# A fused vision block on one core: results with tokens on partitions, one set of value products moved behind the scores, all squares on the vector engine

## The chip, the core and the metric

The kernel runs on one core of a Trainium2 chip. The core has a matrix engine (TensorE, PE in the rows; PEld is its weight load), a vector engine (DVE), a scalar engine (ACT), GpSimd (POOL) and a sync engine (SP) that issues the transfers. The metric is device time in microseconds, the median of several runs. All times in the rows are microseconds from the start of one profiled execution.

## The reference

The input is 32 images of 3x64x64. Each is cut into 16 patches of 768 values, which makes 512 tokens. One block of a transformer follows, all of it in float32:

```python
h = patches @ W.T + b + pos_emb                # 512 x 768 @ 768 x 256
h = h + attention(layernorm(h))                # 16 heads of 16, causal, ALiBi bias, 16 tokens an image
h = h + ffn(layernorm(h))
# ffn: hid = bitlinear(x, w_fc) + gate * (x @ v.T @ fast_b.T @ u.T)     256 -> 1024
#      out = bitlinear(relu(hid) ** 2, w_proj)                          1024 -> 256
# bitlinear(x, w): s = mean(|w|, row); x @ (clip(round(w / s), -1, 1) * s).T
```

`s` of the last `bitlinear` has one value for each of the 256 output features, so it can be multiplied in after the product.

## The kernel before, in words

All 512 tokens are on the chip at once, as four blocks of 128 (`BLOCKS`) in two halves of 256 (`HALVES`, index `f`). Each engine has its program written out by hand, in the order in which it is to run; semaphores join the engines. There is no scheduler: an instruction whose semaphore is late holds everything behind it on its engine.

The order on PE: embedding; transposes of the normalised tokens `z`; key, query and value products of half 0; scores of half 0; key, query and value products of half 1; transposes of `u`; scores of half 1; `values(0)` (probabilities times values); transposes of the rounded weights; `project(0)`; `values(1)`; transposes of `z` and of the residual stream `h2` for half 0; the hidden layer (`hidden`, four steps `j` of 256 features); the output products `mlp_out(f, j)`, with the steps of half 1's hidden layer between them.

Products that need more accuracy than one pass has are split: an operand is held as a high part (`hi`, made by ACT) and a low part (`lo`, made by DVE or POOL by subtraction). So each hidden step `n = 4f + j` is followed by this chain: ACT applies relu and scale to the two PSUM tiles (`relus`); DVE or POOL squares the result in full precision (`square`); ACT makes the rounded square (`squares`, `sq_hi`); the same engine as for `square` subtracts (`square_low`, `sq_lo`); PE multiplies both parts by the weights `mlp_t` (`mlp_out`). POOL does n = 1, 2, 3 and DVE does n = 0, 4, 5, 6, 7 (`SQ_POOL`, `SQ_DVE`).

The result is held with the 256 features on the partitions and the tokens along the row, two tiles for each half. For that PE transposes `h2` of each half (`turn(f, h2, ...)`, line 311), DVE copies it out (`tokens_copy`, line 898), and DVE adds it to the scaled product in one instruction (`result`, line 877), with the scale as a value per partition. The host transposes the array that comes back.

`key_spread` lays the keys of each head of a group of four into their own rows; of the four heads of half 0 ACT does head 0, POOL head 1, DVE heads 2 and 3. `fold_v` (line 407) makes a 256x16 product of the low-rank factors `v` and `fast_b`; ACT copies it to `vf_sb`, and POOL makes `v_fold` from it.

The lines that follow are the functions that the change touches.

Of the kernel before, what the change touches and what calls it, by code (L numbers as in the profile page):

```python
# [7 lines left out]
F32 = mybir.dt.float32  # L8
# [6 lines left out]
P = 128  # L15
# [41 lines left out]
def build_program(nc, head, pos, tail, consts, w_q, w_k, w_v, w_fc, w_mlp, w_proj, proj_bias, u_t0, v_t0,  # L57
                  out_t):
    with ExitStack() as ctx:
# [3 lines left out]
        def sem(name):  # L63
# [16 lines left out]
        vf_sb = sb("vf_sb", [P, KE, RANK])  # L80
# [61 lines left out]
        h2_t = sb("h2_t", [P, HALVES, KE, HT])  # L142
# [8 lines left out]
        out_sb = tail_sb[:, :, :, :].rearrange("p b k t -> p (b k t)")[:, 0:HALVES * KE * HT].rearrange(  # L151
            "p (f m t) -> p f m t", f=HALVES, m=KE)
# [7 lines left out]
        vf_ps = bank[3][:, 0:KE * RANK]  # L160
# [6 lines left out]
        h2t_ps = [bank[3], bank[6]]  # L167
        low_ps = [bank[2][:, 0:HT], bank[4][:, 0:HT]]
        FCB = [bank[i] for i in (0, 1, 2, 0, 5, 1, 2, 0)]
        mlp_ps = [[bank[7][:, m * HT:(m + 1) * HT] for m in range(KE)],  # L170
                  [bank[3][:, 0:HT], bank[6][:, 0:HT]]]
# [32 lines left out]
        vf_done, vf_copied = sem("vf_done"), sem("vf_copied")  # L204
# [46 lines left out]
        h2t_turned = sem("h2t_turned")  # L251
        h2t_ready = sem("h2t_ready")
# [10 lines left out]
        out_ready = sem("out_ready")  # L263
# [6 lines left out]
        SQ_DVE, SQ_POOL = (0, 4, 5, 6, 7), (1, 2, 3)  # L270

        @block.sync
        def _(sp):
# [20 lines left out]
            for f in range(HALVES):  # L294
                for m in range(KE):
                    sp.wait_ge(out_ready, f * KE + m + 1)
                    sp.dma_start(out_t[m * P:(m + 1) * P, f * HT:(f + 1) * HT],
                                 out_sb[:, f, m, :]).then_inc(out_done, 16)
            sp.wait_ge(out_done, 16 * HALVES * KE)

        @block.tensor
        def _(pe):
# [170 lines left out]
            def mlp_out(f, j):  # L473
# [7 lines left out]
                order = [(a, m) for m in range(KE) for a in range(2)] if last else \  # L481
                    [(a, m) for a in range(2) for m in range(KE)]
                for a, m in order:
                    w = mlp_t[:, 2 * j + a, m * P:(m + 1) * P]
# [4 lines left out]
                    if last and a == 1 and m == 0:  # L489
                        mm.then_inc(mlp_tile, 1)  # L490
# [29 lines left out]
            fold_v()  # L520
# [12 lines left out]
            scores(1)  # L533
            pe.wait_ge(ut_ready, 2)
# [7 lines left out]
            pe.wait_ge(duo_ready, 3)  # L542
            project(0)
            turn_mlp(0)
# [4 lines left out]
            turn(0, h2, h2t_ps[0], h2_ready, h2t_turned)  # L549
# [24 lines left out]
            hidden_low(1, 0)  # L574
            hidden_low(1, 1)
# [543 lines left out]
```

## Time and profile before

| | |
|---|---|
| median of 3 runs | 73.71 us (73.63 to 75.11) |
| the profiled execution | 73.37 us, of which its span is 71.4 us |
| PE busy | 62.4 us, 87% |
| DVE busy | 44.5 us, 62% |
| ACT busy | 38.3 us, 54% |
| POOL busy | 31.9 us, 45% |
| granted TensorE clock, mean | 0.996 |

A busy share is an average over stages that have different limits. PE's share of 87% counts a matmul from its start to a modelled end, so neighbouring matmuls overlap in it; the distance between two starts tells more. The two rows for DVE and ACT say nothing on whether they are waited for; that stands in what ended PE's idle times.

### The profile page before, as it was taken

To read this page: it belongs to the slowest core of one execution; us is meant where nothing else is said; L and a number is where in the kernel's file an instruction comes from. 1 tells how busy PE (TensorE), PEld (TensorE's weight loads), DVE (VectorE), ACT (ScalarE), POOL (GpSimd) and SP (SyncE) were. 2 spreads that over 40 slices of the span, in tenths; PEclk is the share of its full clock that TensorE was granted. 3 is DMA by queue.
4 is the path that set the end of the run, shared out by engine and by line. 5 is a ranking of instruction groups with operands and counts; after the bars stand their busy time and mean duration, and the time that the engine had idled before them with its cause. 6 is when DMAs were issued, how large, how long until landed. Compare 5 with 4: busy or idle time off the path is not lost. (4 is left out here: it accounts for less than half of the span.)

```text
span 71.4 us, 2149 instructions
## 1 busy us (share of the span) xinstructions
PE 62.4 (87%) x890; PEld 56.0 (78%) x890; DVE 44.5 (62%) x94; ACT 38.3 (54%) x76; POOL 31.9 (45%) x44
## 2 busy tenths in 40 slices
PE   4999999999899999992969959999965899999840
PEld 3678788889799999991948839979855689999730
DVE  1000059288979849977989964368994216589970
ACT  5200005703859759673499895836660593897000
POOL 7400425898567279997994000000089089100000
PEclk9999999999999999999999999999999999999998
DMA  0999999999400000000000000000000000000044
GB/s 5 274 292 328 375 392 412 409 339 405 173 14 0 9 0 0 0 9 0 9 0 0 14 5 0 0 9 0 0 0 0 0 0 0 0 0 0 9 146 148
DMA packets 3497, 6.74 MB, mean 94 GB/s; under 512 B 400, under 2 KB 1312, under 8 KB 3488
## 3 DMA queue, kind: packets, MB, share of 16 engines
q1 hardware_dynamic: 3488, 6.60, 25.9%
q8 instruction: 7, 0.11, 0.7%
q14 instruction: 2, 0.02, 0.1%
HBM read 6.08 MB, written 0.52 MB: 93 GB/s over the span
## 5 line engine op out<-in xcount | busy, mean ns | idle before, releaser
L486 PE MATMUL psum<-sq_hi,mlp_t 128*128 128x256 f32 x32 | 8.1, 289 | 1.6 <-POOL sq_lo L1015 1.2
L594 ACT ACTIVATE std<-mv,eps_sb 128x1 f32<-128x1 f32 x8 | 2.2, 292 | 13.5 <-DVE mv L774 13.5
L1009 POOL TENSOR_TENSOR kqv_sb<-head_sb 128x512 f32<-128x512 f32 x3 | 3.2, 1062 | 13.5 <-ACT head_sb L720 13.5
L720 ACT ACTIVATE head_sb<-psum,fc_scale 128x256 f32<-128x256 f32 x16 | 6.5, 473 | 2.6 <-PE psum L465 2.6
L486 PE MATMUL psum<-sq_lo,mlp_t 128*128 128x256 f32 x32 | 7.8, 280 | 0.0
L486 PEld LDWEIGHTS psum<-sq_hi,mlp_t 128*128 128x128 f32 x32 | 6.0, 188 | 2.2 <-issue 2.2
L456 PE MATMUL psum<-zt_hi,fc_t 128*128 128x256 f32 x32 | 6.8, 285 | 0.3 <-ACT zt_hi L603 0.3
L770 DVE TENSOR_TENSOR h<-psum,pos_sb 128x256 f32<-128x256 f32 x4 | 1.6, 412 | 8.7 <-PE psum L305 8.7
L456 PE MATMUL psum<-zt_lo,fc_t 128*128 128x256 f32 x32 | 6.6, 279 | 0.0
L305 PE MATMUL psum<-head_sb 128*128 128x256 f32 x24 | 6.4, 431 | 0.0
L305 PEld LDWEIGHTS psum<-head_sb 128*128 128x128 f32 x24 | 5.1, 220 | 1.2 <-DMA head_sb<-head 0.5
L486 PEld LDWEIGHTS psum<-sq_lo,mlp_t 128*128 128x128 f32 x32 | 6.0, 188 | 0.0
L798 DVE TENSOR_TENSOR zt_lo<-psum,zt_hi 128x512 fp32r<-128x512 f32 x4 | 2.8, 691 | 5.2 <-ACT zt_hi L603 5.2
L456 PEld LDWEIGHTS psum<-zt_hi,fc_t 128*128 128x128 f32 x32 | 5.3, 188 | 0.6 <-issue 0.6
L305 PE MATMUL psum<-head_sb,tail_sb 128*128 128x256 f32 x24 | 5.5, 379 | 0.0
L780 DVE TENSOR_SCALAR z<-h,mv,rstd 128x256 f32<-128x256 f32 x8 | 5.2, 655 | 0.3
L456 PEld LDWEIGHTS psum<-zt_lo,fc_t 128*128 128x128 f32 x32 | 5.3, 188 | 0.0
L727 ACT ACTIVATE sq_hi<-head_sb 128x512 fp32r<-128x512 f32 x8 | 5.0, 636 | 0.1
L305 PEld LDWEIGHTS psum<-head_sb,tail_sb 128*128 128x128 f32 x24 | 4.5, 190 | 0.6
L1015 POOL TENSOR_TENSOR sq_lo<-kqv_sb,sq_hi 128x512 fp32r<-128x512 f32 x3 | 3.8, 1278 | 2.3 <-ACT sq_hi L727 2.3
L325 PE MATMUL psum<-zt_hi,kqv_hi 128*128 128x256 f32 x16 | 4.8, 299 | 0.0
L1021 POOL TENSOR_SCALAR fc_whole<-fc_sb,fc_scale 128x256 f32<-128x256 f32 x8 | 4.6, 598 | 0.0
(112 smaller groups left out, 169.4 us busy)
## 6 DMA issues: line engine op xcount, KB each, us to landing
head_sb<-head SPq DMA_DIRECT2D x6, 256.0 KB, 4.7
fc_sb<-w_fc SPq DMA_DIRECT2D x2, 512.0 KB, 6.7
mlp_sb<-w_mlp SPq DMA_DIRECT2D x2, 512.0 KB, 9.0
tail_sb<-tail SPq DMA_DIRECT2D x2, 384.0 KB, 5.8
out_t<-tail_sb SPq DMA_DIRECT2D x4, 128.0 KB, 1.8
pos_sb<-pos SPq DMA_DIRECT2D x1, 256.0 KB, 5.0
kqv_sb<-w_k SPq DMA_DIRECT2D x1, 256.0 KB, 6.0
kqv_sb<-w_q SPq DMA_DIRECT2D x1, 256.0 KB, 6.0
```

The costliest lines, as they stand in the source:

```text
L305: return pe.matmul(tok_ps[b], lhs, head_sb[:, k, HT:HT + E], start=k == 0, stop=k == KF - 1)
L325: mm = pe.matmul(ps[f][:, g * HT:(g + 1) * HT], w, part[f][:, k, :], start=k == 0 and i == 0, stop=k == KE - 1 and i == 2)
L456: pe.matmul(FCB[n][:, a * HT:(a + 1) * HT], fc_t[:, k, m * P:(m + 1) * P], part[f][:, k, :], start=a == 0 and k == 0 and part is z2t_hi, s ...
L486: mm = pe.matmul(mlp_ps[f][m], w, part[:, n % RING, a, :], start=j == 0 and a == 0 and i == 0 and (m == 0 or f == 1), stop=last and a == 1 ...
L594: nc.scalar.activation(std[:, which, b:b + 1], mv[:, which, b, 1:2], ACT.Sqrt, bias=eps_sb[:, 0:1]).then_inc(std_ready, 1)
L720: nc.scalar.activation(relu[:, n % PART_RING, a, :], FCB[n][:, a * HT:(a + 1) * HT], ACT.Relu, scale=fc_scale[:, 0, m:m + 1]).then_inc(rel ...
L727: nc.scalar.activation(sq_hi[:, n % RING, :, :], relu[:, n % PART_RING, :, :], ACT.Square).then_inc(sq_hi_ready, 1)
L780: dve.tensor_scalar(z[:, b, :], hidden_state[:, b, :], mv[:, which, b, 0:1], rstd[:, which, b:b + 1], ALU.subtract, ALU.mult).then_inc(z_s ...
L798: dve.tensor_tensor(dst, src, hi.bitcast(F32), ALU.subtract).then_inc(signal, 1)
L1009: pool.tensor_tensor(sq[:, r, :, :], relu[:, r, :, :], relu[:, r, :, :], ALU.mult).then_inc(sq_pool, 1)
L1015: pool.tensor_tensor(sq_lo[:, n % RING, :, :], sq[:, r, :, :], sq_hi[:, n % RING, :, :].bitcast(F32), ALU.subtract).then_inc(sq_lo_pool, 1)
L1021: pool.tensor_scalar(dst[:, m, :], w[:, m, :], scale[:, 1, m:m + 1], ROUND, ALU.mult, ALU.add).then_inc(signal, 1)
```

## The change

The change has six parts.

1. The result is made with tokens on the partitions. In `mlp_out` the squares are now the stationary operand and the weights move, as many products and of the same shape as before. The transposes of `h2`, DVE's copies of them and the host's transpose go away. The scale now varies along the row, so it needs a tile that has it in every partition: `fold_v_spread_scale` makes it with two float32 products of the broadcast scale with the identity, next to the old `fold_v`, and ACT copies both out together (`side_sb`, 128x288). The last step is two instructions for each of the four blocks: DVE multiplies by the scale, then POOL (blocks 0, 1) or DVE (blocks 2, 3) adds `h2`.
2. `fold_v` moves from before the scores of half 0 to just before `project(0)`, with the two products for the scale.
3. `value(1)` moves from before `turn_u` to between `scores(1)` and `values(0)`.
4. Head 2 of half 0's key spread moves from DVE to POOL; DVE's first `fc_sums` moves ahead of `zt_low(1)`.
5. DVE makes all eight squares and low parts. In half 0 it normalises blocks 2 and 3 first and squares after; in half 1 `square(n + 1)` stands ahead of `square_low(n)`.
6. PE, ACT: transposes of `z` of half 1 stand before `mlp_out(0, 0)`; `mlp_out(0, 1)` stands behind the first hidden step of half 1 and `mlp_out(0, 2)` behind its third. ACT runs `relus(1)` and `squares(1)` ahead of the standard deviations of blocks 2 and 3, and one standard deviation of half 0 ahead of `mlp_signs(0)`.

The diff, cut to its core:

```diff
-        SQ_DVE, SQ_POOL = (0, 4, 5, 6, 7), (1, 2, 3)
+        SQ_DVE, SQ_POOL = (0, 1, 2, 3, 4, 5, 6, 7), ()
...
-            def fold_v():
+            def fold_v_spread_scale():
                 pe.wait_ge(v0_in, 16)
+                pe.wait_ge(mlp_scaled, 1)
                 for k in range(KE):
-                    mm = pe.matmul(vf_ps[:, k * RANK:(k + 1) * RANK], v_sb[:, k * P:(k + 1) * P], v_sb[:, E:E + RANK],
+                    pe.matmul(side_ps[:, k * RANK:(k + 1) * RANK], v_sb[:, k * P:(k + 1) * P], v_sb[:, E:E + RANK],
+                              start=True, stop=True)
+                for m in range(KE):
+                    c = KE * RANK + m * P
+                    mm = pe.matmul(side_ps[:, c:c + P], mlp_scale[:, 0, m:m + 1].broadcast_to([P, P]), ident,
                                    start=True, stop=True)
-                mm.then_inc(vf_done, 1)
+                mm.then_inc(side_done, 1)
...
+                for a, b in order:
                     for i, part in enumerate((sq_hi, sq_lo)):
-                        mm = pe.matmul(mlp_ps[f][m], w, part[:, n % RING, a, :],
-                                       start=j == 0 and a == 0 and i == 0 and (m == 0 or f == 1),
+                        mm = pe.matmul(mlp_ps[f * BH + b], part[:, n % RING, a, b * P:(b + 1) * P],
+                                       mlp_t[:, 2 * j + a, :],
+                                       start=j == 0 and a == 0 and i == 0 and (b == 0 or f == 1),
                                        stop=last and a == 1 and i == 1, skip_group_check=True)
...
             value(0)
-            fold_v()
             score_bias(0)
             scores(0)
             pe.wait_ge(k_copied, 1)
             key(1)
-            pe.wait_ge(vf_copied, 1)
             query(1)
-            pe.wait_ge(q_copied, 1)
-            value(1)
             pe.wait_ge(shift_ready, 1)
             pe.wait_ge(v_copied, 1)
             turn_u()
             score_bias(1)
             scores(1)
+            value(1)
...
             pe.wait_ge(duo_ready, 3)
+            fold_v_spread_scale()
             project(0)
+            pe.wait_ge(side_copied, 1)
             turn_mlp(0)
...
             turn(0, z, z2t_ps[0], z2_ready, z2t_turned)
-            turn(0, h2, h2t_ps[0], h2_ready, h2t_turned)
...
             hidden(0, 3)
+            turn(1, z, z2t_ps[1], z2_ready, z2t_turned)
             pe.wait_ge(mlpt_ready, 2)
             mlp_out(0, 0)
-            mlp_out(0, 1)
-            pe.wait_ge(h2t_ready, 1)
-            turn(1, z, z2t_ps[1], z2_ready, z2t_turned)
-            turn(1, h2, h2t_ps[1], h2_ready, h2t_turned)
             hidden_main(1, 0, (z2t_hi,))
             low_rank(1)
             hidden_main(1, 0, (z2t_lo,))
+            mlp_out(0, 1)
+            hidden_low(1, 0)
+            hidden_main(1, 1)
+            hidden_low(1, 1)
             pe.wait_ge(relu_ready, 6)
-            hidden_main(1, 1)
-            hidden_low(1, 0)
-            hidden_low(1, 1)
+            hidden(1, 2)
             mlp_out(0, 2)
-            hidden(1, 2)
             pe.wait_ge(relu_ready, 8)
             hidden(1, 3)
             mlp_out(0, 3)
...
-            def result(f, m):
-                if f == 1 and m == 0:
+            def scale_result(b):
+                if b < BH:
+                    dve.wait_ge(mlp_step, STEPS)
+                elif b == BH:
                     dve.wait_ge(mlp_tile, 2)
                 else:
-                    dve.wait_ge(mlp_step, STEPS * (f + 1))
-                dve.wait_ge(h2t_ready, f + 1)
-                dve.scalar_tensor_tensor(out_sb[:, f, m, :], mlp_ps[f][m], mlp_scale[:, 0, m:m + 1],
-                                         h2_t[:, f, m, :], ALU.mult, ALU.add).then_inc(out_ready, 1)
+                    dve.wait_ge(mlp_step, 2 * STEPS)
+                dve.wait_ge(side_copied, 1)
+                dve.tensor_tensor(out_sb[:, b, :], mlp_ps[b], scale_row, ALU.mult).then_inc(out_scaled, 1)
+
+            def add_result(b):
+                dve.wait_ge(out_scaled, b + 1)
+                dve.tensor_tensor(out_sb[:, b, :], out_sb[:, b, :], h2[:, b, :], ALU.add).then_inc(out_dve, 1)
```

**Where instructions move.** First PE, from the last key and query products of half 1 to the transposes of the feed-forward weights. L345 (L344 after) is `value(1)`, L371 (L370) the scores, L389 (L388) `values(0)`. Before:

```order
L325 MATMUL psum<-zt_hi,kqv_hi 128x256 [waits zt_hi_ready,q_w_lo,zt_lo_ready,q_w_hi,vf_copied]
...
L345 MATMUL psum<-kqv_hi,zt_hi 128x256 [waits zt_hi_ready,v_w_lo,zt_lo_ready,v_w_hi,q_copied]
...
L415 MATMUL psum<-const_sb,u_fold 128x128 [waits u_step,v_copied,shift_ready]
...
L371 MATMUL psum<-k_spread,q_pad 32x64 [waits k_spread_dve,k_spread_pool,k_spread_act,q_copied]
L371 MATMUL psum<-k_spread,q_pad 32x64 x63
L389 MATMUL psum<-prob_t,v_sb 32x64 [waits v_copied,pt_ready,q_copied,ut_ready]
```

and after:

```order
L419 MATMUL psum<-const_sb,u_fold 128x128 [waits u_step,v_copied,shift_ready]
...
L370 MATMUL psum<-k_spread,q_pad 32x64 [waits k_spread_dve,k_spread_pool,k_spread_act,q_copied]
L370 MATMUL psum<-k_spread,q_pad 32x64 x63
L344 MATMUL psum<-kqv_hi,zt_hi 128x256 [waits zt_hi_ready,zt_lo_ready,v_w_lo,v_w_hi]
...
L388 MATMUL psum<-prob_t,v_sb 32x64 [waits v_copied,pt_ready,q_copied,ut_ready]
```

The twelve value products now stand between the two long runs of small products, and two waits are gone.

Second DVE, from the end of the second normalisation's statistics of block 3 to the low part of half 1's transposed tokens. `kqv_sb<-head_sb` is a `square`, `sq_lo` a `square_low`, `zt_lo` the low part of the tokens, `h_t` the copy of the transposed `h2`. Before:

```order
L774 BN_AGGR mv<-bn 128x2
L887 TENSOR_TENSOR kqv_sb<-head_sb 128x512
L798 TENSOR_TENSOR sq_lo<-kqv_sb,sq_hi 128x512
L778 RECIPROCAL rstd<-std 128x1
L780 TENSOR_SCALAR z<-h,mv,rstd 128x256
L778 RECIPROCAL rstd<-std 128x1
L780 TENSOR_SCALAR z<-h,mv,rstd 128x256
L798 TENSOR_TENSOR zt_lo<-psum,zt_hi 128x512
L868 TENSOR_TENSOR low_t<-psum,low_t 64x256
L898 COPY h_t<-psum 128x512
```

and after:

```order
L773 BN_AGGR mv<-bn 128x2
L777 RECIPROCAL rstd<-std 128x1
L779 TENSOR_SCALAR z<-h,mv,rstd 128x256
L777 RECIPROCAL rstd<-std 128x1
L779 TENSOR_SCALAR z<-h,mv,rstd 128x256
L891 TENSOR_TENSOR kqv_sb<-head_sb 128x512
L797 TENSOR_TENSOR sq_lo<-kqv_sb,sq_hi 128x512
L797 TENSOR_TENSOR zt_lo<-psum,zt_hi 128x512
L891 TENSOR_TENSOR kqv_sb<-head_sb 128x512
L797 TENSOR_TENSOR sq_lo<-kqv_sb,sq_hi 128x512
L867 TENSOR_TENSOR low_t<-psum,low_t 64x256
```

The first square and its low part now stand behind the normalisation of both blocks, and the second pair, which was POOL's, stands between the low part of the tokens and that of the low-rank product.

Third the end of DVE's program, from the last square on. After the change:

```order
L891 TENSOR_TENSOR kqv_sb<-head_sb 128x512
L797 TENSOR_TENSOR sq_lo<-kqv_sb,sq_hi 128x512 x2
L878 TENSOR_TENSOR tail_sb<-psum,side_sb 128x256 x3
L882 TENSOR_TENSOR tail_sb<-tail_sb,h 128x256
L878 TENSOR_TENSOR tail_sb<-psum,side_sb 128x256
L882 TENSOR_TENSOR tail_sb<-tail_sb,h 128x256
```

Before, one group stood behind the last low part: `L877 SCALAR_TENSOR_TENSOR tail_sb<-psum,mlp_scale,h_t 128x256 x4`. Six instructions now follow it on DVE, and two adds run on POOL.

## Rows read from the trace of the kernel before

**Rows 1.** The page: busy us, and granted clock in tenths, 40 slices
```profile
PE 62.4 (87%) x890; PEld 56.0 (78%) x890; DVE 44.5 (62%) x94; ACT 38.3 (54%) x76; POOL 31.9 (45%) x44
...
PEclk9999999999999999999999999999999999999998
```

**Rows 2.** Chain that ended last: start, us, what
```profile
67.48 1.20 PE psum L486 x8
68.70 0.48 DVE tail_sb L877
```

**Rows 3.** Timeline of PE, attention: start, us, engine line op out<-in count [idle before]
```profile
21.19 0.61 PE L407 MATMUL psum<-v_sb 16*128 16x16 f32 x4
21.73 0.39 PE L355 MATMUL psum<-alibi_hi,ident_r 128*128 128x256 f32 x1
...
29.91 1.79 PE L371 MATMUL psum<-k_spread,q_pad 64*32 64x64 f32 x128
31.63 0.74 PE L389 MATMUL psum<-prob_t,v_sb 32*32 32x64 f32 x50
33.80 1.00 PE L389 MATMUL psum<-prob_t,v_sb 32*32 32x64 f32 x78 [1.43 <-issue]
...
37.39 1.97 PE L400 MATMUL psum<-proj_sb,yt 128*128 128x256 f32 x8 [0.69 <-DVE yt L855]
```

**Rows 4.** Timeline of POOL and ACT, keys and queries of half 1
```profile
26.78 1.66 POOL L998 TENSOR_SCALAR k_spread<-k_sb,const_sb 128x512 f32<-128x512 f32 x2 [0.28 <-ACT k_sb L636]
...
27.71 0.83 ACT L629 ACTIVATE q_pad<-psum,const_sb 128x256 f32<-128x256 f32 x2
```

**Rows 5.** Transfer queues between 31.4 and 31.6: packets, MB, share
```profile
q8 instruction: 1, 0.02, 28.7%
```

**Rows 6.** Timeline of DVE: transposes of half 0, softmax of half 1, sum of rows
```profile
29.97 1.30 DVE L850 STREAM_TRANSPOSE prob_t<-prob_n 128x512 f32<-128x512 f32 x2
...
34.96 1.32 DVE L843 SCALAR_TENSOR_TENSOR prob_n<-prob,const_sb,srec 128x512 f32<-128x512 f32 x1
36.47 0.77 DVE L855 TENSOR_TENSOR yt<-y_duo 128x512 f32<-128x512 f32 x1 [0.19 <-ACT y_duo L668]
```

**Rows 7.** Timeline of ACT: a copy of 128x512 from PSUM
```profile
19.88 0.60 ACT L603 ACTIVATE zt_hi<-psum 128x512 fp32r<-128x512 f32 x1
```

**Rows 8.** Timeline, second normalisation of blocks 1 and 3, first relus
```profile
42.31 0.41 DVE L780 TENSOR_SCALAR z<-h,mv,rstd 128x256 f32<-128x256 f32 x1
...
47.49 0.84 ACT L720 ACTIVATE head_sb<-psum,fc_scale 128x256 f32<-128x256 f32 x2 [1.12 <-PE psum L465]
...
52.97 1.26 POOL L1015 TENSOR_TENSOR sq_lo<-kqv_sb,sq_hi 128x512 fp32r<-128x512 f32 x1 [0.25 <-ACT sq_hi L727]
52.98 1.40 DVE L780 TENSOR_SCALAR z<-h,mv,rstd 128x256 f32<-128x256 f32 x1
```

**Rows 9.** Timeline of PE, output products and hidden steps
```profile
51.97 0.36 PE L486 MATMUL psum<-sq_hi,mlp_t 128*128 128x256 f32 x1 [0.21 <-DVE sq_lo L798]
...
54.38 0.36 PE L486 MATMUL psum<-sq_hi,mlp_t 128*128 128x256 f32 x1 [1.23 <-POOL sq_lo L1015]
...
60.92 0.28 PE L456 MATMUL psum<-zt_hi,fc_t 128*128 128x256 f32 x1
...
62.10 0.28 PE L456 MATMUL psum<-zt_hi,fc_t 128*128 128x256 f32 x1
```

**Rows 10.** Timeline of DVE, last squares and low parts
```profile
64.48 0.69 DVE L887 TENSOR_TENSOR kqv_sb<-head_sb 128x512 f32<-128x512 f32 x1
65.26 0.69 DVE L798 TENSOR_TENSOR sq_lo<-kqv_sb,sq_hi 128x512 fp32r<-128x512 f32 x1
65.87 0.68 DVE L887 TENSOR_TENSOR kqv_sb<-head_sb 128x512 f32<-128x512 f32 x1
```

**Rows 11.** Timeline of POOL: one sum of 128x256
```profile
7.66 0.72 POOL L958 TENSOR_TENSOR pos_sb<-pos_sb 128x256 f32<-128x256 f32 x1 [5.12 <-DMA pos_sb<-pos]
```

**Rows 12.** Timeline of PE, the products that run first
```profile
1.05 3.17 PE L495 MATMUL psum<-warm 128*128 128x256 bf16 x14 [1.05 <-DVE warm L751]
```

More of the change, by code:

```diff
@@ L57, in build_program @@
 def build_program(nc, head, pos, tail, consts, w_q, w_k, w_v, w_fc, w_mlp, w_proj, proj_bias, u_t0, v_t0,
-                  out_t):
+                  out):
     with ExitStack() as ctx:
@@ L292, in _ @@
             sp.dma_start(proj_sb[:, :, :], w_proj).then_inc(proj_in, 16)
[L294 to L299, printed above, removed]
+            for b in range(BLOCKS):
+                if b < BH:
+                    sp.wait_ge(out_pool, b + 1)
+                else:
+                    sp.wait_ge(out_dve, b - BH + 1)
+                sp.dma_start(out[b * P:(b + 1) * P, :], out_sb[:, b, :]).then_inc(out_done, 16)
+            sp.wait_ge(out_done, 16 * BLOCKS)
         @block.tensor
@@ L480, in mlp_out @@
                 last = j == STEPS - 1
[L481 to L484, printed above, removed]
+                order = [(a, b) for b in range(BH) for a in range(2)] if last else \
+                    [(a, b) for a in range(2) for b in range(BH)]
+                for a, b in order:
                     for i, part in enumerate((sq_hi, sq_lo)):
-                        mm = pe.matmul(mlp_ps[f][m], w, part[:, n % RING, a, :],
-                                       start=j == 0 and a == 0 and i == 0 and (m == 0 or f == 1),
+                        mm = pe.matmul(mlp_ps[f * BH + b], part[:, n % RING, a, b * P:(b + 1) * P],
+                                       mlp_t[:, 2 * j + a, :],
+                                       start=j == 0 and a == 0 and i == 0 and (b == 0 or f == 1),
                                        stop=last and a == 1 and i == 1, skip_group_check=True)
-                    if last and a == 1 and m == 0:
+                    if last and a == 1 and b == 0:
                         mm.then_inc(mlp_tile, 1)
@@ L690, in _ @@
                 copy_out(u_t[:, i * 512:(i + 1) * 512], ut_ps[i], ut_turned, i + 1, ut_ready)
+            mlp_sums(1)
             value_copy(1)
-            mlp_sums(1)
             exponentials(1)
@@ L732, in _ @@
             squares(0)
+            relus(1)
+            squares(1)
             norm_std(2, 1, var2, std2)
             norm_std(3, 1, var2, std2)
-            relus(1)
             relus(2)
-            squares(1)
+            relus(3)
             copy_out(z2t_hi[1][:, :, :], z2t_ps[1][:, :], z2t_turned, 2, z2t_hi_ready)
             squares(2)
-            relus(3)
+            low_high(1)
             squares(3)
-            low_high(1)
             relus(STEPS)
@@ L910, in _ @@
             normalise1(3)
-            key_spread(0, (2, 3))
+            key_spread(0, (3,))
+            fc_sums(0)
             zt_low(1)
-            fc_sums(0)
             fc_sums(1)
@@ L936, in _ @@
             low_low(0)
-            tokens_copy(0)
             stats2(2)
             stats2(3)
-            square(SQ_DVE[0])
-            square_low(SQ_DVE[0])
             normalise2(2)
             normalise2(3)
+            square(0)
+            square_low(0)
             z2t_low(1)
+            square(1)
+            square_low(1)
             low_low(1)
-            tokens_copy(1)
-            for n in SQ_DVE[1:]:
+            for n in (2, 3):
                 square(n)
                 square_low(n)
-            for f in range(HALVES):
-                for m in range(KE):
-                    result(f, m)
+            square(STEPS)
+            for n in range(STEPS, HALVES * STEPS):
+                if n + 1 < HALVES * STEPS:
+                    square(n + 1)
+                square_low(n)
+            scale_result(0)
+            scale_result(1)
+            for b in (2, 3):
+                scale_result(b)
+                add_result(b)
         @block.gpsimd
@@ L1058, in _ @@
             value_factors()
-            for n in SQ_POOL:
-                square(n)
+            for b in range(BH):
+                add_result(b)
 def shape_constants():
@@ L1114 @@
             for n, t in arrays.items()}
-    out_t = nc.dram_tensor("out_t", (E, TOK), F32, kind="ExternalOutput").ap()
-    build_program(nc, out_t=out_t, **args)
+    out = nc.dram_tensor("out", (TOK, E), F32, kind="ExternalOutput").ap()
+    build_program(nc, out=out, **args)
     got = run_bass_kernel_spmd(nc, [arrays], core_ids=[0])
-    return a(got.results[0]["out_t"]).T.reshape(IMAGES, S, E)
+    return a(got.results[0]["out"]).reshape(IMAGES, S, E)
```

57 lines of the change are left out of this document (20 added, 37 removed).

## The prediction, made before the kernel ran

> **What bounds the kernel now.** I read the page first. PE is busy 87% of the span and no other engine over 62% [rows 1]; this says where to look, not what is waited for. The chain of what ended last tells the end: eight products of `mlp_out(1, 3)` from 67.48, then DVE's last result at 68.70, done at 69.18 [rows 2]. The span is 71.4, so 2.2 us of transfer follow, and 73.37 - 71.4 = 2.0 us lie outside the span. The timeline of PE then shows two kinds of loss: gaps, 1.43 us inside `values(0)` [rows 3] and 1.23 us before `mlp_out(0, 1)`, which waits for POOL's low part [rows 9]; and late starts, since a hand-written order makes each stage begin when the last of its inputs is there. So I carry the change through stage by stage, as a shift of each stage's start. Late work is tied closely: PE steps by 10 products in 1.18 us from one hidden step to the next, 0.118 each [rows 9].
>
> **Attention.** `fold_v` goes from before the scores: from 21.19 to 21.73, -0.54 us [rows 3]. The cover of POOL's second key spread must hold: two spreads take 1.66 [rows 4], and started where one starts now they end some 1.5 us before PE arrives, so this edit and the swap of `fc_sums` cost nothing. `value(1)` goes too: 12 x 0.118 = 1.4. Half 1's scores, at 29.91 [rows 3], could start at 27.97. But then ACT's query copies, done at 28.54 [rows 4], less 0.54, are last: 28.1, a shift of -1.8.
>
> `value(1)` is not saved, it runs behind the scores: `values(0)` starts at 31.63 - 1.8 + 1.4 = 31.2. What it can fill is the gap. The gap opens after 50 of 128 equal rows of one block, with "issue" as its end, so no operand is late [rows 3]; the one instruction packet of that time starts between 31.4 and 31.6, 1.6 us after half 1's scores began [rows 5], and PE goes on at 33.80, 2.3 us later. I take it that PE had run ahead of its own instructions. Then the packet now comes at about 29.8, PE could go on from 32.1, and arrives there at 31.2 + 0.74 = 32.0: 0.1 to 0.2 us of gap instead of 1.43. `values(0)` ends 1.5 us earlier. The Trainium skill (Runtime: NRT & Kernel Launch, Instruction fetch mechanics) says of such refills that PE's store holds 2048 instructions and that the cost of crossing a block is mostly hidden; by that rule the gap is something else and stays. The trace has no row for the store's size, and its gap speaks against "hidden".
>
> Next are the sums of half 0. DVE's softmax of half 1 gains only about 1.0, because DVE itself is busy with half 0's transposes, which ended at 31.27 and gain only the 0.54; its division, at 34.96 with 1.32, comes at 33.95 and ends at 35.3 [rows 6]. `yt`, at 36.47, had waited 0.19 for ACT's rows; these come 1.5 earlier, at 34.9, so DVE is last and `yt` starts at 35.35, -1.1 [rows 6]. In this wait PE does the side products: 0.54 for the old ones, and two float32 products of 128x128. Bounds for those: 0.3 for both if they go as the 0.118 steps with a start each, 0.9 if as the wide projection (1.97 for four products in x8 rows [rows 3]); half the width is nearest, 0.45. They run from 34.9 to 35.9 and `yt` ends at 36.0, so they are hidden, at the worst by 0.4 not. ACT's copy of 128x288 lies between the 128x32 copy that it replaces and the 0.60 of 128x512 [rows 7]; 0.4 by width. It falls before the table load and ACT has that much room before `mlp_signs(0)`. Projection and all up to DVE's statistics of blocks 2 and 3: -1.2, ends -0.8 and -1.4. The transposes of `h2` (half 0) are 0.43 us of PE, but `turn_mlp(1)` behind them waits for ACT's rows anyway: nothing.
>
> **Turning to half 1.** Before, block 3 is normalised at 52.98 in 1.40 us where 0.41 is usual [rows 8]; the POOL subtraction that started with it takes 1.26 and both end together. So POOL held DVE, and it ended at 54.38. POOL is now idle there. ACT's `relus(0)`, at 47.49 [rows 8], comes at 46.3; `squares(0)`, then `relus(1)` (behind the projection of half 1) and `squares(1)` put the last standard deviation at 50.05. Two normalisations take 1.0, so block 3 ends at 51.0: -3.4. The price: `square(0)` now stands behind it. A low part starts 0.78 after its square and lasts 0.69 [rows 10]: 51.0 + 0.78 + 0.69 = 52.5, and `mlp_out(0, 0)`, at 51.97 [rows 9], starts at 52.65, **+0.7**.
>
> **The long stretch.** From there PE has eight output steps of 8 x 0.118 = 0.94, four hidden steps of 1.18 and a low-rank product of 0.47: 12.7 us. I add 0.5: a wait before `mlp_out(0, 1)`, because ACT makes the high part only after `relus(3)`, and DVE needs `zt_lo`, square and low part after it (to 55.3, PE ready at 55.05), and restarts. The last step starts at 52.65 + 12.7 - 0.94 + 0.5 = 64.9 against 67.48 [rows 2]: -2.6. DVE keeps up: behind one another, squares and low parts come every 0.61 to 0.78 [rows 10], which gives the last low part at 64.25, 0.7 before it is needed. The products themselves only swap operands, same count and shape: nothing.
>
> **The tail.** Before, the last result starts 0.02 after the last product ends [rows 2]. Now, with the first tile done at 65.6, DVE runs scale, add, scale, add for blocks 2 and 3. DVE's results of 128x256 last 0.48 [rows 2], about 0.46 apart, 0.5 where one needs the other. 65.65 + 0.5 + 0.45 + 0.5 + 0.45 = 67.55, which is 1.4 after the last product; before it was 0.5: **+0.9**. Blocks 0 and 1 go out by POOL at 0.72 each [rows 11], well before. The Trainium skill (GPSIMD Engine Reference, Key points) says that POOL contends with DVE instructions that read two SBUF inputs, as DVE's adds do; by it the first add could be held up to the end of POOL's second. No row shows two such sums side by side; bounds for the tail, 0.4 (all hidden) to 1.6 (one more sum of 0.72), do not rest on it. Transfers keep their number and size: nothing.
>
> **The sum**, of the profiled execution: -2.6 for the last step's start, +0.9 for the tail, -1.7 in all: 73.37 - 1.7 = 71.7. The median of the runs, 73.71, stands 0.3 above that execution; the forecast is 2.7% below the median. Its own range adds the ends: 71.7 - 0.5 (tail) - 0.3 (no wait in the stretch) - 0.2 = 70.7, and 71.7 + 0.4 (side products) + 0.7 (tail) = 72.8.
>
> **Rivals.**
> - **The gap stays** (it was no refill, or it only moves). For: its releaser is not named, and other refills pass without a gap. Against: it stands inside a run of equal products. `values(0)` then ends 1.2 later than above, but DVE's division already ends at 35.3, so `yt` slips only from 35.35 to 36.1: +0.75, 72.4.
> - **DVE becomes the bound** of the stretch. It has 16 square instructions and two low parts in line from 51.0. For: it carries 3.7 us more than before. Against: 0.7 us of slack by the count above. If each instruction takes 0.1 more (0.77 stands for such a sum beside POOL [rows 6]) 1.8 - 0.7 = 1.1 comes on top: 72.8.
> - **Slower: PE's clock falls** at the turn to half 1. PE has ended `hidden(0, 3)` at 50.6 (51.8 before, 0.2 before the row of 51.97 [rows 9], less 1.2) and waits to 52.65 with four transposes between, its longest pause. The granted clock is full in all slices but the last, after the last product [rows 1], so a pause of 1.43 [rows 3] did not lower it, but one of 2 has no row. At the lower level (1.2 GHz instead of 2.4) 14 products of 256 columns take 3.17, 0.226 each [rows 12] against 0.118, so each us of work takes 1.9. The stretch has 12.7 us of it; from 2.3 us of work on (2.3 x 0.9 = 2.0) the kernel is slower than now: with 2.5 us of work slowed 73.9, with 5 us 76.2.
> - **The change does not do what it says**: scores of half 1 are held by another input, or the standard deviations come late because ACT's `relus(1)` does. Each costs its own shift: up to 1.8 less of the first, with the gap back, 73.3.
>
> **Chances.** The forecast 0.57, gap 0.14, DVE 0.13, clock 0.07, not as said 0.09. A change is told from none at 2%, that is below 72.24 or above 75.18. Some three quarters of the forecast's weight and a fifth of the gap and DVE rivals' lie below 72.24, with 0.1 for a stretch better than counted: faster 0.60. The clock rival's longer half and mishaps behind it lie above 75.18: slower 0.07; the rest, 0.33, within. The range 70.6 to 73.2 takes in the first three cases and part of the fourth; the forecast's own is 70.7 to 72.8.
>
> **What would show it.** Scores of half 1 at 28.1; the gap in `values(0)` under 0.3; `yt` at 35.35; no normalisation over 0.5 on DVE after 45; block 3 normalised by 51.0; `mlp_out(0, 0)` at 52.65 behind DVE's low part; waits of PE after it of 0.5 in all; four DVE instructions, 1.4 us, behind the last product; span 69.7. It is wrong if the gap is still over 1 us, if PE waits for DVE's low parts in half 1, or if a slice of the clock row after 50 is under nine.

## The result, and the profile after

| | before | after |
|---|---|---|
| median of the runs | 74.15 us (73.63 to 75.11, 4 runs) | 70.92 us (70.82 to 72.03, 4 runs) |
| profiled execution, its span | 73.37 us, 71.4 us | 70.84 us, 69.0 us |
| ratio of the runs | | 0.958 (95%: 0.947 to 0.970) |

The change makes the kernel 4.2% faster. The forecast was 71.7 us in 70.6 to 73.2, with a chance of 0.60 for a gain of over 2%; the measured time lies 0.3 us above the lower end of that range. Between the two traces lie 2.5 us, or 3.4%; the rest of the ratio is dealt with under the clock below. Executions of the kernel before come in two groups, with a mean granted clock of about 0.99 or more, or of 0.977 and less, and by their times the four above are two of each.

The page after, busy us and the granted clock in tenths (as [rows 1]):

```profile
PE 61.9 (90%) x886; PEld 55.6 (80%) x886; DVE 45.6 (66%) x99; ACT 38.4 (56%) x76; POOL 25.9 (37%) x41
...
PEclk9999999999999999999999999999999999999997
```

DVE has 1.1 us more work, POOL 6.0 less, and the kernel is shorter: busy shares did not tell what a stage waited for. The timeline of PE after, attention (as [rows 3]), and DVE's sum of rows of half 0 (as [rows 6]):

```profile
28.08 1.79 PE L370 MATMUL psum<-k_spread,q_pad 64*32 64x64 f32 x128
...
31.41 1.77 PE L388 MATMUL psum<-prob_t,v_sb 32*32 32x64 f32 x128
...
35.54 0.71 PE L411 MATMUL psum<-const_sb,mlp_scale 128*128 128x128 f32 x4
36.09 1.89 PE L399 MATMUL psum<-proj_sb,yt 128*128 128x256 f32 x8
```
```profile
35.16 0.68 DVE L854 TENSOR_TENSOR yt<-y_duo 128x512 f32<-128x512 f32 x1
```

Half 1's scores start 1.83 us earlier, and `values(0)` is one piece of 128 rows where it was cut by 1.43 us. This trace runs 0.21 us late before the change can matter (the second transposes of `z` start at 19.62, before at 19.41), so the shifts are 0.2 larger than the times of the two traces show. DVE and PE at the turn to half 1 (as [rows 8, 9]):

```profile
50.58 0.41 DVE L779 TENSOR_SCALAR z<-h,mv,rstd 128x256 f32<-128x256 f32 x1
...
50.91 0.68 DVE L891 TENSOR_TENSOR kqv_sb<-head_sb 128x512 f32<-128x512 f32 x1
51.63 0.69 DVE L797 TENSOR_TENSOR sq_lo<-kqv_sb,sq_hi 128x512 fp32r<-128x512 f32 x1
```
```profile
52.47 0.36 PE L489 MATMUL psum<-mlp_t,sq_hi 128*128 128x256 f32 x1 [0.98 <-DVE sq_lo L797]
...
55.15 0.36 PE L489 MATMUL psum<-mlp_t,sq_hi 128*128 128x256 f32 x1
56.39 0.28 PE L460 MATMUL psum<-zt_hi,fc_t 128*128 128x256 f32 x1
...
57.52 0.28 PE L460 MATMUL psum<-zt_hi,fc_t 128*128 128x256 f32 x1
```

Block 3's normalisation takes 0.41 instead of 1.40 and ends 3.4 us earlier; `mlp_out(0, 0)` starts 0.5 later than before, for the reason forecast, and then PE works on. The tail (as [rows 2]), first DVE, then the last of the chain of what ended last:

```profile
65.22 0.42 DVE L878 TENSOR_TENSOR tail_sb<-psum,side_sb 128x256 f32<-128x256 f32 x1 [0.58 <-PE psum L489]
65.68 0.42 DVE L882 TENSOR_TENSOR tail_sb<-tail_sb,h 128x256 f32<-128x256 f32 x1
66.02 0.42 DVE L878 TENSOR_TENSOR tail_sb<-psum,side_sb 128x256 f32<-128x256 f32 x1
66.47 0.43 DVE L882 TENSOR_TENSOR tail_sb<-tail_sb,h 128x256 f32<-128x256 f32 x1
```
```profile
60.94 4.25 PE psum L489 x36
...
65.22 0.44 DVE tail_sb L878
...
66.47 0.43 DVE tail_sb L882
```

The last product ends at 65.65 and the last result 1.25 us later; before, the two lay 0.5 apart.

### The profile page after: what moved, and what is told of

It is laid out like the page before. It is cut to its first block, busy times and chain, and to the rows that moved or that the text cites. A ratio compares the mean times of both kernels' runs of the same rounds, so it can differ in the third digit from the quotient of the medians.

```text
span 69.0 us, 2144 instructions
## 1 busy us (share of the span) xinstructions
PE 61.9 (90%) x886; PEld 55.6 (80%) x886; DVE 45.6 (66%) x99; ACT 38.4 (56%) x76; POOL 25.9 (37%) x41
## 4 chain that ended last, share of the span: by engine, by line
PE 69%; DVE 12%; ACT 12%; issue 3%
PE psum L304 13%; PE psum L489 11%; PE psum L460 8%; PE psum L370 5%; PE psum L499 5%; PE psum L324 4%; PE psum L344 4%; PE psum L427 3%; PE psum L399 2%; DVE z L779 2%; PE psum L388 2%; PE psum L469 2%; ACT L696 2%; ACT fc_t L614 2%; PE psum L437 2%
## 5 line engine op out<-in xcount | busy, mean ns | idle before, releaser
L1043 POOL TENSOR_TENSOR tail_sb<-tail_sb,h 128x256 f32<-128x256 f32 x2 | 1.4, 732 | 26.3 <-DVE tail_sb L878 26.3
L489 PE MATMUL psum<-mlp_t,sq_hi 128*128 128x256 f32 x32 | 7.9, 285 | 1.1 <-DVE sq_lo L797 1.0
L489 PE MATMUL psum<-mlp_t,sq_lo 128*128 128x256 f32 x32 | 7.7, 281 | 0.0
L489 PEld LDWEIGHTS psum<-mlp_t,sq_hi 128*128 128x128 f32 x32 | 6.0, 189 | 1.5 <-issue 1.5
L489 PEld LDWEIGHTS psum<-mlp_t,sq_lo 128*128 128x128 f32 x32 | 6.0, 189 | 0.0
L891 DVE TENSOR_TENSOR kqv_sb<-head_sb 128x512 f32<-128x512 f32 x8 | 5.4, 686 | 0.7 <-ACT head_sb L719 0.7
L797 DVE TENSOR_TENSOR sq_lo<-kqv_sb,sq_hi 128x512 fp32r<-128x512 f32 x8 | 5.4, 689 | 0.1
```

Source lines behind the costliest of these rows:

```text
L489: mm = pe.matmul(mlp_ps[f * BH + b], part[:, n % RING, a, b * P:(b + 1) * P], mlp_t[:, 2 * j + a, :], start=j == 0 and a == 0 and i == 0 a ...
L797: dve.tensor_tensor(dst, src, hi.bitcast(F32), ALU.subtract).then_inc(signal, 1)
L891: dve.tensor_tensor(sq[:, r, :, :], relu[:, r, :, :], relu[:, r, :, :], ALU.mult).then_inc(sq_ready, 1)
```

## Experiments

Each kernel ran beside the kernel before. The runs on one chip share theirs: 73.96 us (19 runs) for A1 to A4, 73.99 (7 runs) for B1 to C2, 73.74 (7 runs) for D1 to D4. For the result above no chip is on record.

### A1: the value products alone

In the kernel before, only `value(1)` moves, and on ACT its copy goes behind `mlp_sums(1)`, as in the change. What stays as it was: the order at the turn to half 1, POOL's squares, the layout of the result.

```diff
             pe.wait_ge(q_copied, 1)
-            value(1)
...
             scores(1)
+            value(1)
...
-            value_copy(1)
             mlp_sums(1)
+            value_copy(1)
```

> The kernel before, with only the move of value(1) to between scores(1) and values(0) (and mlp_sums(1) ahead of value_copy(1) on ACT, as in the change). Theory (PE ran ahead of its own instructions; value(1) fills the refill): half 1's scores start at 28.6 instead of 29.91, values(0) at 31.8, the gap of 1.43 us inside values(0) is under 0.3, yt comes at about 35.9 instead of 36.47 because DVE is last there, and the time falls by 0.5 us. Rival (the gap is no refill and stays): values(0) ends 0.2 us later than before and the time rises by 0.1 to 0.2 us.

72.80 us (72.68 to 72.95, 4 runs), ratio 0.986 (0.974 to 0.998), span 70.9. PE, then DVE:

```profile
29.00 1.80 PE L371 MATMUL psum<-k_spread,q_pad 64*32 64x64 f32 x128
...
32.33 1.82 PE L389 MATMUL psum<-prob_t,v_sb 32*32 32x64 f32 x128
```
```profile
36.06 0.69 DVE L855 TENSOR_TENSOR yt<-y_duo 128x512 f32<-128x512 f32 x1
...
52.49 1.40 DVE L780 TENSOR_SCALAR z<-h,mv,rstd 128x256 f32<-128x256 f32 x1
```

The gap is gone with this move alone, and `yt` comes 0.4 earlier. The normalisation is still held for 1.40. The two traces lie 0.5 us apart, but A1's runs 0.39 late before the edit can matter (second transposes of `z` at 19.80 against 19.41). With that off, the scores start at 28.61, as expected, and the gain is 0.9 us; the median gives about 1.0 (72.80 against 73.8 for the runs of the kernel before at full clock). The 0.5 expected was too little.

### A2: is the gap a matter of the instruction's number?

The kernel before with 21 more products ahead of everything, that is 42 more instructions of PE's; they are short and unused.

```diff
-            for _ in range(WARM_PRODUCTS):
+            for _ in range(WARM_PRODUCTS - 3):
                 pe.matmul(bank[7][:, 0:HT], warm[:, 0:P], warm[:, :], start=True, stop=True)
+            for _ in range(24):
+                pe.matmul(bank[7][:, 0:16], warm[:, 0:P], warm[:, 0:16], start=True, stop=True)
```

> The kernel before, with 3 of the 14 products at its start replaced by 24 products of 16 columns: 21 products, or 42 PE instructions, more ahead of everything, at about equal time. Nothing that is waited for changes. Theory (refill of PE's instructions, a fixed number of them apart): the gap of 1.43 us moves forward by 21 rows, from behind row 50 of 128 of values(0) to behind row 29, and keeps its length within 0.2 us. Rival (the gap belongs to the work at that place): it stays behind row 50. Time within 0.3 us of the kernel before for both.

74.90 and 76.62 us (2 runs, with a mean granted clock of 0.975 and 0.977). PE:

```profile
31.92 0.38 PE L389 MATMUL psum<-prob_t,v_sb 32*32 32x64 f32 x29
34.03 1.24 PE L389 MATMUL psum<-prob_t,v_sb 32*32 32x64 f32 x99 [1.73 <-issue]
35.20 3.52 PE L423 MATMUL psum<-const_sb,fc_whole 128*128 128x128 f32 x16
```

The gap moved from behind row 50 to behind row 29: 21 rows earlier, each a weight load and a product, for 42 instructions put in front. So the gap stands at a place in PE's instruction stream, whatever is computed there. A count in the traces says the same: when PE stops, it has started 468 products and 469 weight loads in the kernel before, in A2 and in A3 alike. The part on the time failed: the gap lasted 1.73 instead of 1.43, and the transposes behind it (16 products of 128 columns) took 3.52 us instead of 1.97. Each line gives a stretch, its length, the busy time of PE, weight loads, DVE, ACT and POOL, then the granted clock (the last two numbers are transfers):

```profile
34.00:35.00 1.00, 0.97 (x98) 0.97 (x98) 0.82 (x2) 0.11 (x1) 1.00 (x2) 1.00 0.00 0
35.00:36.00 1.00, 1.00 (x27) 0.85 (x11) 0.96 (x2) 0.69 (x2) 1.00 (x2) 0.51 0.09 16
...
37.00:38.00 1.00, 1.00 (x6) 1.00 (x5) 1.00 (x2) 0.73 (x1) 0.93 (x2) 0.50 0.00 0
38.00:39.00 1.00, 1.00 (x8) 0.95 (x6) 0.97 (x3) 0.56 (x2) 0.60 (x2) 0.78 0.00 0
```

PE stood still until 34.03, worked for a us at full clock, and was then granted half of it, the 1.2 GHz level, for 3.4 us (to 38.44).

### A3: the changed kernel with `value(1)` back in its old place

```diff
             query(1)
+            pe.wait_ge(q_copied, 1)
+            value(1)
...
             scores(1)
-            value(1)
...
-            mlp_sums(1)
             value_copy(1)
+            mlp_sums(1)
```

> The changed kernel with value(1) back ahead of turn_u, and value_copy(1) ahead of mlp_sums(1). Theory: half 1's scores at 29.5 instead of 28.08, a gap of 1.4 us again inside values(0), ACT's rows 1.2 us later, yt at 36.05 instead of 35.16, all behind it 0.9 later: 71.8 us. Rival (no gap comes back, only the later scores count): yt 0.6 later, 71.5 us. Second rival (the slack of later stages swallows it): 70.9 us.

Ten runs, in two groups: five at full clock, 71.53 to 72.57 (median 72.13, +1.2 us on the changed kernel), and five with a mean granted clock of 0.946 to 0.976, 74.25 to 75.75 (median 74.53). PE in a run of the second group:

```profile
31.25 0.77 PE L388 MATMUL psum<-prob_t,v_sb 32*32 32x64 f32 x54
33.97 1.09 PE L388 MATMUL psum<-prob_t,v_sb 32*32 32x64 f32 x74 [1.95 <-issue]
34.99 3.41 PE L427 MATMUL psum<-const_sb,fc_whole 128*128 128x128 f32 x16
```

The gap is back, 4 rows later than before; `fold_v` with its 8 instructions no longer runs ahead of it, which is those 4 rows. The instruction packet of that time starts at 31.7, and PE goes on 2.3 us later. The granted clock falls 0.6 us after that (lines as in A2), again for 3.4 us:

```profile
34.00:35.00 1.00, 1.00 (x75) 0.83 (x74) 0.93 (x3) 0.00 (x0) 1.00 (x2) 0.79 0.00 0
35.00:36.00 1.00, 1.00 (x8) 1.00 (x6) 0.89 (x1) 0.90 (x2) 0.35 (x1) 0.50 0.06 16
```

`yt` starts at 36.73, 1.57 later than after the change (0.14 of it is a late start) and 0.7 later than expected; the gap is 1.95 where 1.4 was expected.

### A4: the changed kernel with squares 1 to 3 on POOL

```diff
-        SQ_DVE, SQ_POOL = (0, 1, 2, 3, 4, 5, 6, 7), ()
+        SQ_DVE, SQ_POOL = (0, 4, 5, 6, 7), (1, 2, 3)
...
             z2t_low(1)
-            square(1)
-            square_low(1)
             low_low(1)
-            for n in (2, 3):
-                square(n)
-                square_low(n)
```

POOL's program has the same squares and low parts ahead of its adds.

> The changed kernel with squares and low parts of steps 1, 2 and 3 back on POOL, everything else as in the change. Theory (what the move to DVE buys is that POOL does not hold DVE's normalisation): z of block 3 takes 0.8 to 1.4 us again instead of 0.41, mlp_out(0, 0) starts 0.6 later, the wait before mlp_out(0, 1) goes, and the time rises by 0.4 to 0.6 us to 71.4. Rival (DVE's load bounds the long stretch): with three pairs less DVE the time falls by 0.3 us or more. Second rival: POOL's low parts come too late, as before, with a PE wait over 1 us before mlp_out(0, 1) or (0, 2): 72 us or more.

74.00 us (72.25 to 74.62, 10 runs). Expected were 71.4. Nine of the ten had a granted clock of 0.966 to 0.976 and a median of 74.06; the one at full clock took 72.25. The trace is of the nine; POOL and DVE, then PE and the clock of the page:

```profile
50.71 1.41 POOL L1017 TENSOR_TENSOR sq_lo<-kqv_sb,sq_hi 128x512 fp32r<-128x512 f32 x1
52.09 1.08 POOL L1011 TENSOR_TENSOR kqv_sb<-head_sb 128x512 f32<-128x512 f32 x1
...
51.11 1.17 DVE L779 TENSOR_SCALAR z<-h,mv,rstd 128x256 f32<-128x256 f32 x1
52.20 1.52 DVE L891 TENSOR_TENSOR kqv_sb<-head_sb 128x512 f32<-128x512 f32 x1
```
```profile
PEclk9999999999999999999999999999995599999997
...
54.59 0.36 PE L489 MATMUL psum<-mlp_t,sq_hi 128*128 128x256 f32 x1 [1.82 <-DVE sq_lo L797]
```

POOL holds the normalisation (1.17 for 0.41) and then also `square(0)` on DVE (1.52 for 0.68), a product whose two operands are in SBUF. So `mlp_out(0, 0)` comes 2.1 us later than in the changed kernel; 0.5 of this is older than the edit's first effect, since half 1's first residual sum is as late (47.64 against 47.11). PE's wait there is 1.82, and of the 3.1 us from 51.50 to 54.59 PE works 0.44. The clock falls 0.3 us after it has gone on, for 3.4 us. That is the rival of the prediction that ended slower, in another kernel than the one it was written for.

### D4: the same with the wait filled

A4 with ten unused products of 256 columns right ahead of `mlp_out(0, 0)`.

```diff
             pe.wait_ge(mlpt_ready, 2)
+            for _ in range(10):
+                pe.matmul(bank[6][:, 0:HT], warm[:, 0:P], warm[:, :], start=True, stop=True)
             mlp_out(0, 0)
```

> The kernel with the squares of steps 1, 2 and 3 on POOL, and ten products of 128x128 with 256 columns without use before mlp_out(0, 0), in PE's pause of 1.82 us. Theory (nine of its ten runs were slower because the granted clock fell in that pause): the products take 1.1 to 1.2 us of it, the clock stays full in every run, and the median falls from 74.0 to 72.3 us. Rival (POOL itself makes the runs slow): 74 us as before, or 0.1 more.

This ran on the chip of D1 to D3, not on that of A4. 72.63 us (72.21 to 72.73, 4 runs), ratio 0.983 (0.977 to 0.989), all four at full clock. The wait there is filled for 1.26 us, and 0.73 of it is left:

```profile
52.46 1.26 PE L568 MATMUL psum<-warm 128*128 128x256 bf16 x10
54.45 0.36 PE L489 MATMUL psum<-mlp_t,sq_hi 128*128 128x256 f32 x1 [0.73 <-DVE sq_lo L799]
```

`mlp_out(0, 0)` starts as good as when it did in A4 (0.14 earlier), and the kernel is 1.4 us faster. What changed is that the clock stayed up. That it stayed up because the wait was filled is likely and not shown: none of the 7 runs of the kernel before on this chip had a lowered clock, against 7 of 19 on A4's, and A4 itself did not run here. Of A4's 3.1 us, 1.3 to 1.7 is where the squares run (A4's full-clock run less 70.92 is 1.3, D4 less D1 on one chip 1.4, D4 less 70.92 1.7), and the rest is the clock.

### B1: the add of block 2 on POOL

```diff
-            for b in (2, 3):
-                scale_result(b)
-                add_result(b)
+            scale_result(2)
+            scale_result(3)
+            add_result(3)
```

POOL adds block 2 behind blocks 0 and 1, and SP waits for POOL's add before that transfer.

> The changed kernel with the add of block 2 on POOL, so that DVE runs scale(2), scale(3), add(3) at the end and POOL runs three adds. Theory A (POOL and DVE do not hold one another with two SBUF sums side by side): POOL's third add runs from 65.85 to 66.6, DVE's add(3) from 66.15 to 66.57 in 0.42 us, and the time falls by 0.3 us to 70.5. Theory B (DVE's sum of two SBUF operands is held until POOL's instruction ends): add(3) takes 0.8 us or more and ends at 67.0, and the time stays or rises by 0.1.

71.19 us (71.05 to 71.29), ratio 0.963 (0.957 to 0.969). Neither expectation came as it stood: no gain of 0.3, and the sum on DVE is lengthened, but not to 0.8. DVE:

```profile
65.36 0.90 DVE L878 TENSOR_TENSOR tail_sb<-psum,side_sb 128x256 f32<-128x256 f32 x2 [0.59 <-PE psum L489]
66.29 0.62 DVE L882 TENSOR_TENSOR tail_sb<-tail_sb,h 128x256 f32<-128x256 f32 x1
```

DVE has one sum less to do, but the one left lasts 0.62 instead of 0.43 beside POOL's, so it ends at 66.91, where the changed kernel ends at 66.90.

### B2: `square(0)` and `mlp_out(0, 0)` first

```diff
             hidden(0, 3)
-            turn(1, z, z2t_ps[1], z2_ready, z2t_turned)
             pe.wait_ge(mlpt_ready, 2)
             mlp_out(0, 0)
+            turn(1, z, z2t_ps[1], z2_ready, z2t_turned)
...
+            square(0)
+            square_low(0)
             normalise2(2)
             normalise2(3)
-            square(0)
-            square_low(0)
-            z2t_low(1)
             square(1)
+            z2t_low(1)
             square_low(1)
```

> The changed kernel with DVE's square(0) and square_low(0) ahead of the normalisation of blocks 2 and 3 again, where DVE waits 0.65 us for ACT, PE's mlp_out(0, 0) ahead of turn(1, z), and square(1) ahead of half 1's zt_lo. Theory (PE's start of the long stretch is set by the chain normalisation, square, low part): mlp_out(0, 0) starts at 50.8 instead of 52.47, turn(1, z) at 52.0, hidden_main(1, 0) at 53.0 instead of 53.47, mlp_out(0, 1) at 54.75 instead of 55.15, and the time falls by 0.4 us to 70.4. Rival (the later normalisation delays half 1 as much as the earlier product gains): 70.9, no change.

70.78 us (70.39 to 70.89), ratio 0.956 (0.949 to 0.964). `mlp_out(0, 0)` starts at 50.98 instead of 52.47, but the next hidden step then waits for the tokens of half 1:

```profile
50.98 0.35 PE L489 MATMUL psum<-mlp_t,sq_hi 128*128 128x256 f32 x1 [0.20 <-DVE sq_lo L797]
...
53.36 0.71 PE L460 MATMUL psum<-zt_hi,fc_t 128*128 128x256 f32 x4 [0.78 <-ACT zt_hi L602]
```

The 0.94 us of output products now fill PE's pause, but much of it comes back as this wait. Its trace already runs 0.33 late at the first normalisation's transposes (19.95 against 19.62). With 0.33 taken off, the hidden step starts at 53.03 against 53.47, and the last result, at 66.88, ends at 66.55 against 66.90, so 0.35 earlier; 0.4 was expected. Against 70.92 the median shows 0.1, and against B1 on the same chip 0.4. The medians of the changed kernel differ by 0.3 from chip to chip (D1), so the medians do not settle it.

### C1 and C2: the changed kernel with the old layout of the result

C1 has the features on partitions again: `h2` turned by PE and copied by DVE, and one DVE instruction per result tile. Its other parts are those of the changed kernel. C2 is C1 with the order of B2.

```diff
-            for b in (2, 3):
-                scale_result(b)
-                add_result(b)
+            for f in range(HALVES):
+                for m in range(KE):
+                    result(f, m)
...
+            turn(0, h2, h2t_ps[0], h2_ready, h2t_turned)
...
+            turn(1, h2, h2t_ps[1], h2_ready, h2t_turned)
```

> The changed kernel with the old layout of the result: weights stationary, h2 transposed by PE and copied by DVE, one result instruction a tile, the host transposes; everything else of the change stays (the side products too, whose scale row is then not read). Theory (the transposes and copies lie in waits, the new layout only lengthens the tail from 0.5 to 1.25 us): last result 0.5 us behind the first product's end as before the change, no product later by more than 0.1, and the time falls by 0.7 us to 70.1. Rival (the transposes and copies cost what they are busy, 0.43 us of PE and 0.69 us of DVE in each half): the time rises to 71.3 or stays.

> Both of the last two edits: old layout of the result, and square(0) with mlp_out(0, 0) first. Theory: the two gains lie in different stretches and add, but for the second transposes of h2, which now stand ahead of hidden_main(1, 0) and take 0.43 us of PE in a wait of about the same length: 69.8 us. Rival: the transposes lie on the path there, 70.2 us. PE's longest pause falls under 1.3 us and the granted clock stays full in every run.

C1: 70.43 us (70.17 to 70.83), ratio 0.954 (0.947 to 0.961), expected 70.1. C2: 70.37 (70.14 to 70.57), ratio 0.952 (0.946 to 0.959), expected 69.8: the second gain is not seen. PE at the turn and DVE at the end of C1:

```profile
51.20 0.60 PE L313 MATMUL psum<-const_sb,h 128*128 128x128 f32 x4
52.34 0.36 PE L493 MATMUL psum<-sq_hi,mlp_t 128*128 128x256 f32 x1 [0.55 <-DVE sq_lo L804]
```
```profile
65.19 0.95 DVE L883 SCALAR_TENSOR_TENSOR tail_sb<-psum,mlp_scale,h_t 128x256 f32<-128x256 f32 x2 [0.59 <-PE psum L493]
```

The transposes of half 1's `h2`, 0.60 us, lie in PE's wait for the low part; the results end at 66.14 instead of 66.90. C1's trace is 0.12 early at the second transposes of `z` (19.50 against 19.62), which leaves 0.64, as expected.

### D1 to D3: the same, again, on one chip

The changed kernel, C1 and C2, without an edit, so that the differences of half a us are seen twice.

> The changed kernel again, unedited, for comparison on this chip: 70.9 us, the granted clock full until the last product in every run.

> The old layout of the result on the changed kernel, again, beside the changed kernel on one chip. Theory (only the tail differs): 0.6 to 0.7 us less than the changed kernel. Rival (the 0.5 us between them so far is the chip or the start of the run): within 0.2 us.

> Old layout and square(0) first, again. Theory: 0.1 to 0.3 us less than the old layout alone, since half 1's first hidden step starts 0.3 us earlier and DVE's last squares, which wait for ACT's relus, hardly do. Rival: no difference.

D1: 71.25 us (70.64 to 71.67). D2: 70.21 (69.85 to 71.08). D3: 70.34 (69.58 to 70.56). The ratios to before are 0.965 (0.957 to 0.973), 0.955 (0.946 to 0.964) and 0.951 (0.944 to 0.959). The old layout is faster than the new one by 1.0 us on this chip (D2 against D1) and by 0.5 in C1 against 70.92. The traces of D1 and D2 say 0.66 (last results at 66.58 and 65.81, less 0.11 at the start), nearly what C1's says. D3 is not told from D2 by the medians; in its trace the last result is 0.36 earlier. The best kernels measured are C1 and C2, at a ratio of 0.951 to 0.955 against 0.958 to 0.965 for the change; the intervals overlap.

## Why the prediction was right

By its own steps:

- **Scores and the gap** (right). Scores of half 1: forecast 28.1, measured 28.08 (27.87 with the late start off). `values(0)`: 31.2, measured 31.41. The packet: 29.8, measured between 29.6 and 29.8. The gap: 0.1 to 0.2, measured 0.3 (128 rows in 1.77, where `values(1)` takes 1.47 for as many). A2 shows that its place goes by the count of PE's instructions, A1 and A3 that the place of `value(1)` decides it: between the two runs of small products it takes time in which, as I read it, the next instructions come. No row shows the refill itself, only the packet and the place. What one argument rested on was looser than it looked: from the packet's start to PE's going on are 2.3 us before, 2.3 in A3 and 2.9 in A2. The Trainium skill (Runtime: NRT & Kernel Launch, Instruction fetch mechanics) says that the cost of crossing a block is mostly hidden. The runs show an exception: 1.4 to 2.0 us in the open, where the 128 scores with their weight loads, 256 instructions, are used up in 1.79 us. At the same count of instructions PE stops for 0.3 us in C2 and in D4.
- **The sum of half 0** (right). `yt`: 35.35, measured 35.16. The side products last from 35.00 to 36.09 with the old ones, and `yt` is done at 35.84. Before, the projection started 0.15 after `yt` was done, now 0.25: hidden but for 0.1. ACT's copy took 0.41, forecast 0.4.
- **The turn to half 1** (right). Block 3 normalised: 51.0, measured 50.99. `mlp_out(0, 0)`: 52.65, measured 52.47. That POOL held the normalisation is shown by A4, where it does so again (1.17). A4 adds what neither the prediction nor A4's expectation had for the turn: POOL holds DVE's `square` of two SBUF operands as well (1.52). The Trainium skill (GPSIMD Engine Reference, Key points) says that POOL contends with such instructions. The prediction had used this for the tail alone, and there B1 shows 0.2 us.
- **The stretch** (right, 0.2 too long). The last step starts at 64.55, forecast 64.9. Half of the difference is the start at 52.47. The 0.5 for waits was about right, and between 55.2 and 58.6 the products came every 0.113 instead of 0.118. DVE kept up: its one wait for ACT in the squares of half 1 is 0.68, before 61.93, so the rival with DVE as the bound did not come.
- **The tail** (right in kind, mis-sized by 0.15). 1.4 us behind the last product, measured 1.25: results of 128x256 take 0.42, not 0.48, and start 0.34 to 0.46 apart.
- **The total**: 71.7 against 70.84, 0.86 too high; between the traces the forecast gain was 1.7 us and the measured one 2.5, or 2.7 with the late start off. The terms all err to one side: 0.35 at the start of the last step, 0.3 from there to the last result (66.90 against 67.55), and 0.2 in what follows it and lies outside the span.

**The clock** is where the prediction was right by luck in part. It read from one trace with a full clock [rows 1] that a pause of 1.43 does no harm, and gave the clock a chance only in the new pause. In 9 of the 33 runs of the kernel before that stand beside the experiments the mean granted clock is 0.977 or less, and these have a median of 74.8 against 73.8 for the other 24. A2 and A3 show such a fall in their traces, 1.0 and 0.6 us behind this gap. One such stretch, 3.4 us at half clock in a span of 72, makes a mean of 0.976, which is what the nine runs have (0.972 to 0.977). In A1, with the gap gone, four runs of four kept full clock, which alone could be chance on a chip where 12 of 19 runs of the kernel before kept it too. But so did the changed kernel's eight, and all 40 runs of the kernels whose traces have no pause of over 1.3 us, A1 and D4 among them. The wait of 1.23 us before `mlp_out(0, 1)` [rows 9] is still in A1 (1.22), so it is not the one that counts. That the gap also lowers the clock in the nine runs of before is inferred; none of them left a trace. If so, the change gives 2.5 us (D1 against the kernel before on its chip) to 2.9 us in undisturbed runs (73.8 against 70.92), and removes a further 1.0 us that about a quarter of the runs paid. By chip these were 7 of 19, 2 of 7 and 0 of 7, so the chip or the time of the run has a part in it that no run separates. What stays open is why 1.43 to 1.95 us of pause lower the clock in some runs and not in others. The pause that the rival named (PE with four transposes from 50.53, then idle for 0.98 until 52.47) never did so, and A4, with 1.82 us of idle there, had a lowered mean clock in 9 runs of 10. The last slice of the clock row after the change, 7, lies behind the last product, as the 8 before did.

**The parts of the gain.** The move of `value(1)` is worth 0.9 to 1.0 us alone (A1) and 1.2 in the changed kernel (A3, full clock). Squares 1 to 3 on DVE, in the changed order, are worth 1.3 to 1.7 at full clock (A4's one run, D4). The move of `fold_v`, the key spread and the orders of parts 5 and 6 did not run alone. The new layout takes back 0.5 to 1.0 by the medians and 0.65 by the traces (C1, D1 and D2): what it removes, the transposes and copies of `h2`, lay in waits of PE, and what it adds lies behind the last product. The prediction had both halves of this (the transposes as nothing, the tail as +0.9) without drawing the conclusion, that the change is better without its first part.

## What to carry to other kernels

Cost a moved piece by the wait that it fills or leaves, and by what it puts behind the last product, not by its own length. Where PE pauses for some 1.4 us or more, look at the granted clock of several runs, not at one trace, and try to fill the pause, with unused products if nothing real can be put there (D4: ten of them, -1.4 us, on another chip than A4). In these traces POOL was free only for work beside which DVE had no normalisation and no sum or product of two SBUF operands.

## What the runs showed of the hardware

- PE can stop for 1.43 to 1.95 us with no operand late. The place moves with the number of instructions ahead of it (21 rows for 42 instructions), and 12 real products between two long runs of tiny ones hide all but 0.3 us of it. That PE waits for its own instructions is the reading that fits both.
- After a pause the granted clock fell to its 1.2 GHz level 0.3 us (A4), 0.6 (A3) and 1.0 (A2) after PE had taken up work again, and stayed there for 3.4 us in all three traces. Runs with a lowered mean were longer by 1.0 us (before), 1.8 (A4, against its one run at full clock) and 2.4 (A3).
- DVE beside one instruction of POOL: a normalisation of 128x256 takes 1.17 to 1.40 instead of 0.41, a product of two SBUF operands of 128x512 1.52 instead of 0.68, a sum of 128x256 0.62 instead of 0.43 (before and A4, A4, B1).
